# Weighted values of two head sets at a time, at two places of an attention body instead of four, with a third buffer of probabilities

## What is computed

```python
q, k, v = proj(layernorm(x)), proj(ctx), proj(ctx)   # 16 heads of 8
logits = q @ k.T / sqrt(8)            # layer 1: + mask * -1e9
attn = softmax(logits)                # [8, 16, 256, 256]
out = (attn @ v) @ Wo + bo            # "weighted values", then a projection
x = x + out
```

## Time and profile before

| | |
|---|---|
| median of 3 runs | 593.12 us (593.01 to 593.52) |
| the profiled execution | 592.77 us, of which 590.7 us are its span |
| TensorE matmul busy | 489.0 us (83%) |
| VectorE busy | 364.9 us (62%) |
| ScalarE busy | 308.3 us (52%) |
| GpSimd busy | 182.4 us (31%) |
| weighted values, line 1494 | 68.5 us for 1024 instructions |
| exponentials, line 902 | 147.1 us for 256 instructions |

### The profile page before, as it was taken

The page is one execution under the profiler, slowest core; times in us unless marked ns, Lnnn a source line. Parts: engine busy times, 40 slices in busy tenths (PEclk is TensorE's granted clock), DMA queues, the critical chain, the costliest instruction groups (busy, mean ns, idle before and its releaser), DMA issues.

```text
span 590.7 us, 12613 instructions
## 1 busy us (share of the span) xinstructions
PE 489.0 (83%) x3970; PEld 403.7 (68%) x3970; DVE 364.9 (62%) x1266; ACT 308.3 (52%) x659; POOL 182.4 (31%) x405
## 2 busy tenths in 40 slices
PE   2447899899997899963599999999999899599980
PEld 1336677767775688752477877777777778499980
DVE  7886687677873066675667778678687653312203
ACT  2214677667766444542146666666566355245550
POOL 7230012222122121101100112452443347775550
PEclk9998999999999999996659999999999999979995
DMA  6304432334305950004134324333321530132107
GB/s 178 110 16 128 128 100 83 96 106 127 89 31 232 412 179 2 1 0 137 46 105 122 106 68 136 95 93 120 103 76 47 166 95 28 52 98 76 47 18 213
DMA packets 52264, 60.02 MB, mean 102 GB/s; under 512 B 7633, under 2 KB 43354, under 8 KB 50928
## 3 DMA queue, kind: packets, MB, share of 16 engines
q1 hardware_dynamic: 49936, 55.09, 30.3%
q0 software_dynamic: 2272, 4.24, 2.2%
HBM read 30.01 MB, written 29.23 MB: 100 GB/s over the span
## 4 chain that ended last, share of the span: by engine, by line
PE 45%; DVE 8%; issue 6%; ACT 3%; DMA 3%; POOL 3%; SPq 0%; DVEq 0%; POOLq 0%; ACTq 0%
PE ps L1530 6%; PE ps L1494 5%; PE ps L1545 5%; PE ps L1548 5%; PE ps L1733 5%; PE ps L1723 5%; PE ps L1686 1%; PE ps L1557 1%; PE ps L1459 1%; PE ps L1461 1%; PE ps L1460 1%; PE ps L1447 1%; DVE ps L1142 1%; DMA k_blocks<-y_dram 1%; POOL ln_rstd L434 1%
## 5 line engine op out<-in xcount | busy, mean ns | idle before, releaser
L902 ACT ACTIVATE probs<-ps 128x512 f32<-128x512 f32 x256 | 147.1, 598 | 89.9 <-PE ps L1548 86.2
L1530 PE MATMUL ps<-k_blocks,q_stacks 128*128 128x256 f32 x512 | 122.1, 325 | 19.1 <-DVE row_max L1134 7.9
L1142 DVE CUSTOM_DVE_ANT_0 ps<-ps,mask_q 128x256 f32<-128x256 f32 x256 | 102.4, 452 | 35.6 <-PE ps L1530 34.6
L1548 PE MATMUL ps<-q_stacks,k_blocks 128*128 128x256 f32 x512 | 106.7, 292 | 0.6 <-DMA q_stacks<-maxT 0.3
L1134 DVE TENSOR_REDUCE row_max<-ps 128x2 f32<-128x512 f32 x128 | 84.2, 686 | 33.3 <-PE ps L1530 32.0
L1530 PEld LDWEIGHTS ps<-k_blocks,q_stacks 128*128 128x128 f32 x512 | 83.6, 203 | 27.5 <-DVE row_max L1134 12.1
L1548 PEld LDWEIGHTS ps<-q_stacks,k_blocks 128*128 128x128 f32 x512 | 88.1, 191 | 20.2 <-issue 10.1
L1494 PE MATMUL ps<-probs,v_aug 128*32 128x256 f32 x1024 | 68.5, 385 | 6.0 <-ACT probs L902 3.7
L773 POOL TENSOR_SCALAR max_split<-row_max 128x16 fp32r<-128x16 f32 x32 | 6.5, 204 | 187.1 <-DVE row_max L1134 78.2
L1545 PE MATMUL ps<-mask_k,neg_mask_eye 128*128 128x512 f32 x128 | 55.0, 430 | 0.0
L718 POOL DMA_INDIRECT y_dram<-x_ring x39 | 40.9, 1047 | 23.5 <-ACT x_ring L999 19.5
(11 more groups left out here) (208 smaller groups left out, 825.0 us busy)
## 6 DMA issues: line engine op xcount, KB each, us to landing
slots_dram<-x_ring SPq DMA_DIRECT2D x1, 10400.0 KB, 29.9
q_stacks<-q_dram SPq DMA_DIRECT2D x32, 256.0 KB
q_dram<-qk_parts SPq DMA_DIRECT2D x16, 384.0 KB, 3.7
k_dram<-qk_parts SPq DMA_DIRECT2D x16, 384.0 KB, 4.0
k_blocks<-k_dram SPq DMA_DIRECT2D x128, 48.0 KB
raw<-L_ffn_fc_w SPq DMA_DIRECT2D x12, 256.0 KB, 4.4
x_ring<-slots_dram SPq DMA_DIRECT2D x39, 65.0 KB, 1.9
ctx_in<-ctx SPq DMA_DIRECT2D x16, 128.0 KB, 2.2
```

The source lines that it names most:

```text
L902: eng.activation(probs[:, n // HPS % 2, n % HPS, :, :].rearrange("p k q -> p (k q)"), ps[:, head_bank(BANKS_T, n)[0], :], ACT.Exp).then_in ...
L1142: last = eng.tensor_tensor_reduce(out=scored, in0=scored, in1=mask_q[1 - r][:, i, :], scale=1.0, scalar=-3.0e38, op0=ALU.add, op1=ALU.max, ...
L1530: mm = eng.matmul(ps[:, bank, i * S:(i + 1) * S], q_stack[r][:, st, i * P:(i + 1) * P], k_blocks[r][:, st, j, :], start=True, stop=True)
L1548: mm = eng.matmul(ps[:, bank, k * S:(k + 1) * S], k_blocks[r][:, st, j, k * P:(k + 1) * P], q_stack[r][:, st, :], start=(l == 0), stop=(l ...
```

## The change

The four places of `weighted_v` become two, each with two sets one behind the other: sets 0 and 1 of batch `b` at step 9 of body `b`, sets 2 and 3 of batch `b` at step 1 of body `b+1`. The last two sets of layer 1 stand ahead of the expert part. The probabilities get a third buffer: sets 0, 1, 2, 3 use buffers 0, 1, 2, 1. Stages move by a step: in layer 0 outT from 2 to 3 and normT from 5 to 6, in both layers ScalarE's copy of the second half of the output (`a_out1`) from step 0 to 1 and `d_norm` from 3 to 4, in layer 0 `a_norm` from 6 to 7.

```diff
-    "pv": (5, 5),
+    "pv": (1, 1),
...
-    "outT": (2, 3),
-    "normT": (5, 7),
+    "outT": (3, 3),
+    "normT": (6, 7),
...
-    "a_out1": (0, 0),
+    "a_out1": (1, 1),
...
-    "a_norm": (6, 7),
+    "a_norm": (7, 7),
...
-    "d_norm": (3, 3),
+    "d_norm": (4, 4),
...
-        probs = sb("probs", [P, 2, HPS, NT, S])
+        PROBS = (0, 1, 2, 1)
+        probs = sb("probs", [P, 3, HPS, NT, S])
...
-                        if n % HPS == 0 and (n >= 8 or after(b, 0)):
-                            eng.wait_ge(a.pv, b * 4 + n // HPS - 1)
+                        st = n // HPS
+                        if n % HPS == 0 and st < 3 and after(b, 0):
+                            eng.wait_ge(a.pv, b * 4 - (2, 0, 1)[st])
+                        if n == 3 * HPS:
+                            eng.wait_ge(a.pv, b * 4 + 2)
...
-                    if n % HPS == at["pv"] % HPS:
-                        if n == at["pv"] % HPS:
-                            if exists(b - 1):
-                                weighted_v(eng, l, b - 1, 1 - r, 3)
-                        elif exists(b):
-                            weighted_v(eng, l, b, r, (n - at["pv"]) // HPS)
+                    if n == at["pv"] and exists(b - 1):
+                        for st in (2, 3):
+                            weighted_v(eng, l, b - 1, 1 - r, st)
+                    if n == at["pv"] + H // 2 and exists(b):
+                        for st in (0, 1):
+                            weighted_v(eng, l, b, r, st)
...
-            weighted_v(eng, 1, NB - 1, 1, SETS - 1)
+            for st in (2, 3):
+                weighted_v(eng, 1, NB - 1, 1, st)
```

More of the change, by code:

```diff
@@ L899, in body @@
                         eng.wait_ge(a.t_ps, b * 16 + n + 1)
-                        if n % HPS == 0 and (n >= 8 or after(b, 0)):
-                            eng.wait_ge(a.pv, b * 4 + n // HPS - 1)
-                        eng.activation(probs[:, n // HPS % 2, n % HPS, :, :].rearrange("p k q -> p (k q)"),
+                        st = n // HPS
[3 more added lines that the diff above has]
+                            eng.wait_ge(a.pv, b * 4 + 2)
+                        eng.activation(probs[:, PROBS[st], n % HPS, :, :].rearrange("p k q -> p (k q)"),
                                        ps[:, head_bank(BANKS_T, n)[0], :], ACT.Exp).then_inc(a.p_sb, 1)
@@ L1494, in weighted_v @@
                     mm = eng.matmul(ps[j * HR:(j + 1) * HR, bank, col:col + S], v_aug[r][:, k, st * HPS + j, :],
-                                    probs[:, st % 2, j, k, :], start=(k == 0), stop=(k == NT - 1),
+                                    probs[:, PROBS[st], j, k, :], start=(k == 0), stop=(k == NT - 1),
                                     tile_position=(0, j * HR))
```

## The result

The changed kernel takes 619.0 us (median of 4 runs, 618.37 to 623.21), beside 593.32 us for the kernel before on the same chip: 1.0438 times as long, interval 1.0403 to 1.0474. The forecast was 607.0 us with a range of 596 to 617. The direction and the loop through memory are as forecast; the size is not, and the range missed by 2 us.

A forecast was written before the change was run, and what follows sets the result against it. In layer 0 TensorE, VectorE and a loop through memory were taken as limits within some 0.3 us of each other. Terms 11.5 + 4.5 - 1.8 = 14.2 us over 592.77 gave 607.0 us, range 596 to 617.

The forecast's parts named there:

- the loop through memory: Layer 0: body start, q and k products, `qk_lo`, write, load, next start; 8.63 + 9.23 = 17.86 us, the whole body.
- The drain: TensorE's entries and exits at 32-column matmuls: a merge saves 0.30 us, 16 merges in each layer, 9.6 us if alone.
- Layer 0's five bodies: Layer 0, bodies 1 to 5: write at 11.3 us, bodies of 20.5 against 18.19 us, 2.3 each, +11.5 us.
- the placement: Layer 0: new body's first half laid on the old; q and k start about 6.15, 1.0 us later than TensorE could.
- second limit: Layer 0: without the loop through memory, VectorE's maxima still let the next body start at 20.1 us at the earliest.
- Layer 1's bodies: Layer 1: value product at 11.1 us after waiting about 1.5; +0.9 us a body, five bodies, +4.5 us.
- The rest ... there I let the merges count: Layer 0's body 6 and layer 1's bodies 6 and 7, without new q and k: 3 x 0.6 = -1.8 us.
- the sum: Whole kernel: 11.5 + 4.5 - 1.8 = 14.2 us over the profiled execution's 592.77.
- the drains count: Rival, 10%: ScalarE and VectorE catch up in the long pair, the waits do not form; 592.8 - 9.6 = 583 us.
- More backlog: Rival, 6%: half 1 loads or ScalarE's late exponentials add 1 us to each of ten bodies; 617 us.
- the three bodies of that rival: Clock rival, 4%: longer waits at `qk_lo` lower the clock; three bodies with matmuls near 30 us give 645 us.

The follow-up runs named there:

- loop_cut: The changed kernel with layer 0's context copy at step 1, low parts of q and k at step 4 and `head_norm` at step 5; 617.6 us.
- l1_old: The changed kernel with layer 1's moved stages put back, layer 0's kept moved and both pairs kept; 619.0 us.
- v_late: The changed kernel with layer 1's value product and ScalarE's copy of it one step later; 621.1 us.
- top_late: The changed kernel with layer 1's `router_top` directly behind the low parts of q and k, still in step 4; 621.8 us.
- l0_old: The changed kernel with layer 0's moved stages put back, layer 1's kept moved and both pairs kept; 609.8 us.
- split: The changed kernel with pairs pulled apart: set 2 at step 1, set 3 at 2, set 0 at 9, set 1 at 10; 630.7 us.
- set3_early: The kernel before with the third buffer and layer 0's set 3 at step 0, not step 1; sets alone, old stages; 593.2 us.
- best: The kernel before with the third buffer, layer 0's set 3 at step 0 and layer 1's `router_top` behind the low parts; 589.7 us.
- pairs_old_steps: The changed kernel with the moved stages put back in both layers, both pairs and the third buffer kept; 607.0 us.

## Why the prediction was right in direction and wrong in size

- **The drain, 0.30 us a merge, pair 1.86 us:** right. The pair measured 1.87, and 30 pairs pulled apart lost 11.7 us against 9.0, with sets moved by a step in it.
- **Layer 0's five bodies, +11.5 us:** right, +11.9, with some luck in the number. Write at 11.78 us and not 11.3, then 9.09 and not 9.23. The forecast was placed on the body that begins at 106.91, which had waited 1.47 us for its loads and so entered its set 1.68 us after its start. The next body of the kernel before, from 124.77 on, enters it after 2.07 us, as the changed kernel does:

```profile
126.84 1.07 PE L1494 MATMUL ps<-probs,v_aug 128*32 128x256 f32 x16
```

  Against that body (18.11 us, its write at 9.04) the write came 2.74 us later and the body is 2.76 us longer. Five times that would be 13.8. It came to 11.9 because the first of the five grew by 2.0 only, and because the third had the wait of 1.47 us in the kernel before and not in this trace of the changed one. The wait for the context copy (0.87 us) is where the placement had it. VectorE's longest wait is ahead of step 4 (2.52 us); the text had named the one ahead of step 2, which is 2.07. By experiment the context copy is 0.9 us of a body. The forecast's second limit, VectorE at 20.1 us, fits loop_cut, which removed 2.4 us from the way to the write while the body stayed at 20.7; that kernel also moved `head_norm`, so it does not single this limit out.
- **Layer 1's bodies, "A body is +0.9 us", +4.5 us:** right mechanism, sized too small. The wait ahead of the value product is 1.53 us as forecast, but the product starts 11.36 us after the body's first scores and not 11.1 (10.61 before). Behind it TensorE waits for VectorE's maxima twice more (0.32 and 0.26 us), where the forecast put 0.4 us. It measured 1.4 us a body over the bodies 2 to 5, and +6.6 us with the first bodies.
- **"The rest ... there I let the merges count", -1.8 us:** this step failed. It measured +7.2 us: +0.7 ahead of the five bodies, +3.2 in the rest of layer 0, -0.3 up to layer 1, +2.9 in layer 1's bodies 6 and 7, +0.7 behind them. That is 9.0 of the 11.5 us by which the sum was short. I took bodies without new q and k for bodies without a chain that binds. They still have raw scores, VectorE's maxima, the output copy and `head_norm` on the way. TensorE in layer 0's last body:

```profile
193.20 0.51 PE L1552 MATMUL ps<-q_stacks,k_blocks 128*128 128x256 f32 x2 [0.85 <-DMA q_stacks<-maxT]
...
194.85 3.19 PE L1498 MATMUL ps<-probs,v_aug 128*32 128x256 f32 x32
...
199.73 1.06 PE L1690 MATMUL ps<-ident,o_raw 128*128 128x128 f32 x8 [0.79 <-ACT o_raw L978]
...
203.47 0.71 PE L1705 MATMUL ps<-wo,o_normT 128*128 128x128 f32 x4 [0.69 <-ACT o_normT L922]
```

  Both output stages wait for ScalarE behind the pair. The pair itself takes 3.19 us there and not 1.93 for another reason, which is no part of the order of the stages: the granted clock. Over the pair it was 0.59, a mix of the 1.2 and 2.4 GHz levels, after TensorE had waited 0.85 and 0.24 us shortly before:

```profile
194.85:197.97 3.12, 3.12 (x34) 1.34 (x33) 0.00 (x0) 0.59 (x1) 1.72 (x3) 0.59 0.06 21
```

  l1_old has the same code in layer 0, and there the clock stayed up:

```profile
195.18 1.93 PE L1501 MATMUL ps<-probs,v_aug 128*32 128x256 f32 x32
```

  The rest of layer 0 takes 45.9 us in l1_old, v_late and top_late, which have the same order there at the full clock. So of the +3.2 us 1.5 are the order's and about 1.6 the clock's in this one execution. The six kernels with old stages and a third buffer, l0_old with both pairs among them, take 44.3 to 44.5 us there, 45.0 with the pair at step 1 alone: the 1.5 us are the moved stages' and not the pairs'. In layer 1's bodies 6 and 7, at the full clock in both kernels, 1.8 of the 2.9 us are the pairs' (46.8 us in l1_old against 45.0), the other 1.2 the moved stages'. Even without the clock's part this term measured +5.6 us where the sum had -1.8.
- **The rivals:** "the drains count" falls, although the drains are real. The clock stayed up in both bodies that are shown (1.00) and fell once in the attention of layer 0, for the pair above, which is far from the three bodies of that rival. "More backlog", 617 us, is nearest in its number alone: it priced 1 us more in each of the ten bodies, and the ten came out 2.5 us over the sum together; what was missing lay outside them.

What stays open: how split's loss divides into drains, the later places of two sets and the clock, how much the moved stages cost in layer 1, and the +0.7 us ahead of the five bodies and behind layer 1's bodies.

The Trainium skill, "Trainium Kernel Development and Optimization", section "Best Practices", says that TensorE tiling speeds up compute but not the evacuation of PSUM. The tiling is the same before and after, so no run here tests the first half. The second fits: TensorE's sets took 5.2 us less, VectorE's reading of the scores out of PSUM took as long as before (84.2 and 85.0 us in layer 0) and only began later.

## What to carry to other kernels

In this kernel TensorE is busy 97% of a body and feeds VectorE, and there a long block on the first leaves the second without work: merging two 1 us blocks saved 0.3 us on TensorE and made the wait of VectorE behind them 0.9 us longer (1.20 to 2.07 us in layer 0, 2.09 to 2.95 in layer 1), which it could not make up. Ask of a piece of work that is to be moved what wait it fills where it stands (set 0 ahead of the value product), and count a loss in every body that has the same chain, also at the ends of a loop where the obvious term is missing. Test a pair of edits in both orders: here the moved stages cost 12 us with the pairs and 38 without.

## What the runs showed of the hardware

- One body of layer 0 differs from one execution to the next, and a single profile hides it. set3_early and best have the same code there; their five bodies take 92.7 and 88.9 us (writes of q from 61.42 to 154.09, and from 61.83 to 150.70). 3.2 of the 3.8 us are one body, the third of the five, and it has two causes. In set3_early it waits 2.00 us for the loads, in best not at all; and behind that wait the granted clock was 0.61 up to 112.00 (1.00 in best), so that a set takes 1.94 us and not 1.07:

```profile
107.89 0.79 PE L1534 MATMUL ps<-k_blocks,q_stacks 128*128 128x256 f32 x2 [2.00 <-DMA k_blocks<-k_dram]
108.61 1.94 PE L1501 MATMUL ps<-probs,v_aug 128*32 128x256 f32 x16
```

  The 1.47 us of the earlier trace rows is the same wait, and there the clock stayed at 1.00. The profiled execution of l0_old has both in its third body, and its five bodies take 96.8 us where pairs_old_steps, the same code, takes 94.1. A difference of under 4 us in layer 0 is read from medians, not from two traces.
- The first scores behind a wait are dearer: in the layer 0 body above, scores take 0.24 us to the next start when they stand directly behind other scores (140.67 to 140.91) and 0.34 behind a wait of 0.16 (142.74 to 143.08). A wait is not needed for most of it: behind transposes that run without a gap it is 0.32 (140.11 to 140.43).
